# Gated delta layer and gated MLP on one core: weights kept for eight steps, a ring of four places for k, 32x32 blocks through DRAM, and a first phase of three stages with two sets of tiles

## The reference

```python
x = x + layernorm(attn(layernorm(x)))
x = x + layernorm(mlp(layernorm(x)))

# attn, 32 heads, key and value width 64
q, k, v, z = split(x @ w_qkvz.T);  b, a = split(x @ w_ba.T)
q, k, v = causal_conv4(q, k, v)            # depthwise, 4 taps
g = -exp(A_log) * softplus(a + dt_bias);   beta = sigmoid(b)
q = l2norm(q) / 8;  k = l2norm(k)
for t in range(256):                       # state S: 64 x 64 per head
    S = S * exp(g[t])
    S = S + outer(k[t], (v[t] - k[t] @ S) * beta[t])
    o[t] = q[t] @ S
out = (rmsnorm(o) * norm_weight * sigmoid(z)) @ w_out.T
# mlp
out = (silu(h @ w_gate.T) * (h @ w_up.T)) @ w_down.T
```

## Time and profile before

| | |
|---|---|
| runs | 3611.32, 3615.00, 3629.64 us; median 3615.0 |
| profiled execution | 3628.41 us, its span 3626.6 us |
| first phase | 0 to about 159 us |
| second phase | about 169 to 3235 us |
| third phase | to the end |
| busy share of the span | PE 91%, PEld 61%, DVE 69%, ACT 49%, POOL 30% |
| mean granted PE clock | 0.961 of full speed |
| moved by DMA | 351 MB in 930,158 packets, 857,712 of them under 512 bytes |

### The profile page before, as it was taken

One profiled execution on the slowest core, in us unless ns is written; L12 is line 12 of the kernel. 1 busy time (PEld: TensorE's weight loads), 2 busy tenths in 40 slices (PEclk: granted clock), 3 DMA queues, 4 the chain that ended last, 5 costly groups with the idle time before them and its releaser, 6 DMA issues. The chain is left out here.

```text
span 3626.6 us, 117234 instructions
## 1 busy us (share of the span) xinstructions
PE 3284.2 (91%) x51008; PEld 2221.8 (61%) x51008; DVE 2486.1 (69%) x5826; ACT 1769.1 (49%) x3338; POOL 1093.2 (30%) x902
## 2 busy tenths in 40 slices
PE   4489999999999999999999999999999999869998
PEld 2246666666666666666666666666666666645554
DVE  5467767777777777777777777776776777635555
ACT  2245555555555555555555545554555555423333
POOL 0043333333333333333333333333333333300000
PEclk7689999999999999999999999999999999969999
DMA  2235445444544444444444444444444454320000
GB/s 76 75 91 112 113 112 113 113 113 113 113 113 104 103 108 108 106 104 112 104 113 113 113 113 113 113 113 103 110 113 91 109 115 98 87 71 18 24 24 18
DMA packets 930158, 351.24 MB, mean 97 GB/s; under 512 B 857712, under 2 KB 878576, under 8 KB 921328
## 3 DMA queue, kind: packets, MB, share of 16 engines
q1 hardware_dynamic: 929648, 343.73, 40.3%
HBM read 240.35 MB, written 61.34 MB: 83 GB/s over the span
## 5 line engine op out<-in xcount | busy, mean ns | idle before, releaser
L1134 PE MATMUL bank<-xT,w_sb 128*128 128x512 f32 x2048 | 1023.0, 623 | 22.0 <-DMA w_sb<-in_w_qkvz 17.5
L678 POOL TENSOR_TENSOR kq<-kq,products 128x510 f32<-128x510 f32 (+2 forms) x384 | 445.0, 1165 | 941.9 <-ACT kq L752 656.6
L1134 PEld LDWEIGHTS bank<-xT,w_sb 128*128 128x128 f32 x2048 | 350.3, 190 | 309.5 <-issue 253.6
L930 DVE SCALAR_TENSOR_TENSOR kq<-bank,cw,kq 128x510 f32<-128x510 f32 (+2 forms) x384 | 286.6, 746 | 203.9 <-ACT kq L752 189.3
L666 POOL TENSOR_TENSOR dec_a<-gcrow,gccol 128x1024 f32<-128x1024 f32 x64 | 121.8, 1904 | 1001.1 <-DMA beta<-beta_d 1001.1
L1162 PE MATMUL bank<-kq 64*64 64x128 f32 x4096 | 280.7, 278 | 13.2 <-issue 11.4
L930 DVE SCALAR_TENSOR_TENSOR v_c<-bank,cw,v_c 128x510 f32<-128x510 f32 (+2 forms) x384 | 285.2, 743 | 9.0
L948 DVE TENSOR_TENSOR x_un<-x_un,prod_un 128x15 f32<-128x15 f32 (+7 forms) x960 | 258.1, 269 | 32.9
L944 DVE TENSOR_TENSOR prod_un<-a_un,x_un 128x15 f32<-128x15 f32 (+7 forms) x960 | 255.8, 266 | 29.9 <-DMA a_un<-a_d 3.3
L1255 PE MATMUL bank<-wo,u_sq 128*128 128x256 f32 x1024 | 261.4, 399 | 2.8 <-DVE u_sq L1007 2.8
L1162 PEld LDWEIGHTS bank<-kq 64*64 64x64 f32 x4096 | 237.2, 137 | 19.1 <-issue 19.1
(11 more groups left out here) (135 smaller groups left out, 6148.2 us busy)
## 6 DMA issues: line engine op xcount, KB each, us to landing
w_sb<-in_w_qkvz SPq DMA_DIRECT2D x64, 1024.0 KB, 7.9
xT<-xT_d SPq DMA_DIRECT2D x64, 512.0 KB, 5.4
gcrow<-gcrow_d SPq DMA_DIRECT2D x128, 256.0 KB, 5.5
a_d<-a_mat SPq DMA_DIRECT2D x128, 256.0 KB, 3.9
k_old<-kq SPq DMA_DIRECT2D x64, 512.0 KB, 3.8
z_t<-z_d SPq DMA_DIRECT2D x128, 256.0 KB, 4.6
x_row<-x_d SPq DMA_DIRECT2D x128, 256.0 KB, 4.5
wo<-in_w_out SPq DMA_DIRECT2D x64, 256.0 KB, 3.2
```

The source lines that it names most:

```text
L678: nc.gpsimd.tensor_tensor(t[:, :, d:SEQ], t[:, :, d:SEQ], prod[:, :, 0:SEQ - d], ALU.add).then_inc(tap_added[i], 1)
L930: ins = nc.vector.scalar_tensor_tensor(t[:, :, d:SEQ], src[:, :, 0:SEQ - d], cw[:, w:w + 1], t[:, :, d:SEQ], ALU.mult, ALU.add)
L1134: ins = nc.tensor.matmul(bank[:, :], w_sb[:, h, s * P:(s + 1) * P], xT[:, h, :], start=(h == 0), stop=(h == HT - 1))
```

## The change

1. **Weights.** `w_two`, `cw_two` and `wo` have two places, by the parity of the head group. `weights(g)` loads all three once per group, issued two steps before the group starts (group 0 in the first phase). `scale_wo` runs once per group. `xT` has two places too, and `load_x` loads it alone, with no wait of its own.
2. **k.** `kq` becomes one tile of six planes: k of step m in plane m mod 4, q in plane 4 + m mod 2. `keep_k` and `k_old` are gone; `key_state` reads k where it was written, and `scores` takes k and q with a stride between planes.
3. **Blocks.** The scratch tensors `a_d`, `z_d`, `x_d` hold only the 32x32 diagonal blocks. `units_out`, `z_back` and `x_back` are four DMAs each instead of two, with rows of 32 floats (128 bytes), for `x_back` 16 rows of 16 floats per block; `units_in`, `z_out` and `x_out` are one DMA instead of two, and `x_out` stores only the upper 16x16 block of each 32x32. gccol and beta come in one DMA (`gcb`).
4. **First phase.** `spans` runs 10 turns; in turn t, span t is normalised, span t - 1 is projected and gets its gates, and span t - 2 is turned and summed. Most tiles have two places (the banks of the turned x too). beta is computed on ACT as `exp(-ln(1 + exp(-b)))` with a clamp on DVE; the copies of beta to `btc` move from DVE to ACT. The load of x is issued ahead of the constants. Zeros are stored to `z_d` only, at the start; POOL clears `z_t` and `x_row` in SBUF. The first weights are loaded in this phase.

```diff
@@ second phase, SP
+                    def weights(g):
+                        if g > 1:
+                            for k in range(2):
+                                sp.wait_ge(op_full[k], NSP * (g - 1))
+                        sp.dma_start(w_two[g % 2][:, :, :].rearrange("p h t -> p (h t)"), w_qkvz[g]).then_inc(w_in, 16)
+                        sp.dma_start(cw_two[g % 2][:, :], conv_w[g]).then_inc(cw_in, 16)
+                        sp.dma_start(wo[g % 2][:, :, :].rearrange("p a h -> p (a h)"), w_out[g]).then_inc(wo_in, 16)
+
+                    def load_x(m):
+                        sp.dma_start(xT[m.par][:, :, :].rearrange("p h t -> p (h t)"), xT_d[m.index() % NSP]).then_inc(x_T_in[m.par], 16)
+                        if m.off % NSP == NSP - 2 and m.grp + 1 < NHG:
+                            weights(m.grp + 1)
...
                     def units_out(m):
-                        for h in range(2):
-                            sp.dma_start(whole(a_d, h), a_mat[m.par][D * h:D * h + D, :, :]) \
-                                .then_inc(a_d_out, 16)
+                        for q in range(4):
+                            c = W2 * (q % 2)
+                            sp.dma_start(rows32(a_d, q), a_mat[m.par][W2 * q:W2 * q + W2, :, c:c + W2]).then_inc(a_d_out, 16)
...
                     def z_back(m):
-                        for h in range(2):
-                            sp.dma_start(z_t[m.par][D * h:D * h + D, :, :], whole(z_d, h)).then_inc(z_in, 16)
+                        for q in range(4):
+                            c = W2 * (q % 2)
+                            sp.dma_start(z_t[m.par][W2 * q:W2 * q + W2, :, c:c + W2], rows32(z_d, q)).then_inc(z_in, 16)
...
                     def x_back(m):
-                        for h in range(2):
-                            sp.dma_start(x_row[D * h:D * h + D, :, :], whole(x_d, h)).then_inc(x_row_in, 16)
+                        for q in range(4):
+                            c = W2 * (q % 2)
+                            sp.dma_start(x_row[W2 * q:W2 * q + B, :, c:c + B], rows32(x_d, q)[0:B, :, 0:B]).then_inc(x_row_in, 16)
...
                     def turn(s):
                         if s[3]:
                             identity_in(s[3])
-                        if s[2]:
-                            wait_for(sp, conv_done[5], s[2], 1, back=1)
-                            wait_for(sp, tap_done[5], s[2], 1, back=1)
-                            load_cw(s[2])
-                        if s[3]:
                             wait_for(sp, mats_done[0], s[3], 1)
                             units_out(s[3])
                         if s[2]:
                             wait_for(sp, qg_done[1], s[2], 1, back=1)
                             load_gates(s[2])
                         if s[3]:
-                            wait_for(sp, a_d_out, s[3], 32)
+                            wait_for(sp, a_d_out, s[3], 64)
                             units_in(s[3])
                             wait_for(sp, zt_done, s[3], 1)
                             z_out(s[3])
-                            load_wo(s[3])
-                            keep_k(s[3])
                             x_out(s[3])
-                            wait_for(sp, z_d_out, s[3], 32)
+                            wait_for(sp, z_d_out, s[3], 16)
                             z_back(s[3])
-                            wait_for(sp, x_d_out, s[3], 32)
+                            wait_for(sp, x_d_out, s[3], 16)
                             x_back(s[3])
                         if s[1]:
-                            wait_for(sp, proj_full[7], s[1], 1, back=1)
-                            load_xw(s[1])
+                            load_x(s[1])
@@ second phase, places of k and q
+            def half_of(m, q):
+                return kq[:, 4 + m.par if q else m.off % 4, :, :]
```

More of the change, by code:

```diff
@@ L175, in gated_delta_sandwich @@
         sp_gate = sem("sp_gate")
+        w_in, cw_in, wo_in = (sem(n) for n in ("w_in", "cw_in", "wo_in"))
         pool_gate = sem("pool_gate")
@@ L217, in gated_delta_sandwich, with spans @@
+            def spans(turn):
+                for t in range(TURNS):
+                    turn(t if t < NSP else None, t - 1 if 0 <= t - 1 < NSP else None, t - 2 if t >= 2 else None)
             with nc.Block() as block:
@@ L273, in _ @@
[L273 removed]
+                    sp.dma_start(w_two[0][:, :, :].rearrange("p h t -> p (h t)"), w_qkvz[0]).then_inc(w_in, 16)
+                    sp.dma_start(cw_two[0][:, :], conv_w[0]).then_inc(cw_in, 16)
+                    sp.dma_start(wo[0][:, :, :].rearrange("p a h -> p (a h)"), w_out[0]).then_inc(wo_in, 16)
+                    sp.wait_ge(zeros, 3)
+                    for q in range(4):
+                        sp.dma_start(rows32(z_d, q), z_t[0][W2 * q:W2 * q + W2, :, 0:W2]).then_inc(zeros_out, 16)
@@ new lines, in turn @@
+                    def turn(j, k, i):
+                        if j is not None:
+                            if 1 <= j < NSP - 1:
+                                load(j + 1)
+                            store_norm(j)
+                        if i is not None:
+                            store_gates(i)
+                    spans(turn)
+                    sp.wait_ge(eye_in, 32)
+                    sp.wait_ge(zeros_out, 64)
+                    sp.wait_ge(const_in, CONSTS)
+                    for i in range(2):
+                        sp.wait_ge(xT_out[i], 8 * NSP)
+                        sp.wait_ge(col_out[i], 16 * NSP)
+                        sp.wait_ge(row_out[i], 8 * NSP)
@@ new lines, in betas, with rows @@
+                    def betas(i):
+                        act.wait_ge(tok_copied, i + 1)
+                        wait(act, col_out[i % 2], 32 * (i // 2))
+                        for h in range(2):
+                            half = slice(D * h, D * h + D)
+                            nc.scalar.copy(btc[i % 2][half, :, :], tok[i % 2][half, :, h:NH:2].rearrange("p c h -> p h c"))                                 .then_inc(btc_copied, 1)
+                    def rows(i):
+                        act.wait_ge(gc_ready, 2 * i + 2)
+                        wait(act, row_out[i % 2], 16 * (i // 2))
+                        nc.scalar.copy(gcr[i % 2], banks[5][0:NH, :]).then_inc(row_copied, 1)
@@ new lines, in turn @@
+                    def turn(j, k, i):
+                        if k is not None:
+                            magnitudes(k)
+                        if j is not None:
+                            turned(j)
+                        if i is not None:
+                            betas(i)
+                        if k is not None:
+                            gates(k)
+                        if i is not None:
+                            rows(i)
+                        if j is not None and j < NSP - 1:
+                            deviations(j + 1)
@@ L378, in rows @@
-                    def rows(i):
-                        act.wait_ge(gc_ready, 2 * i + 2)
-                        wait(act, row_out, 16 * i)
-                        nc.scalar.copy(gcr, banks[5][0:NH, :]).then_inc(row_copied, 1)
-                    def turn(i):
-                        gates(i)
-                        deviations(i + 1)
-                        turned(i + 1)
-                        rows(i)
-                    deviations(0)
-                    turned(0)
-                    turn(0)
@@ L392, in _ @@
-                    for i in range(1, NSP - 1):
-                        turn(i)
-                    gates(NSP - 1)
-                    rows(NSP - 1)
+                    spans(turn)
                 @block.tensor
```

441 lines of the change are left out of this document (214 added, 227 removed).

## The result

The kernel after takes 3399.74 us (median of 4 runs, 3395.45 to 3404.11) beside 3622.32 us for the kernel before on the same chip (4 runs, 3611.32 to 3630.67). The ratio is 0.9387, with a 95% interval of 0.9354 to 0.9421. The profiled execution took 3400.17 us, its span is 3398.1; against the 3628.41 of before that is 228 us less, where I forecast 169. Direction and order of the parts were right, and the time lies in the range, but only 5 us above its lower end of 3395: the size was too small by 59 us, and the time is nearly that of the rival *all gaps go* (3393), which had a chance of 0.12.

A forecast was written before the change was run, and what follows sets the result against it. Chained engines bound the first phase, PE the second; 3628.4 - 70 (first phase) - 7 (junction) - 92 (second-phase loads) = 3459. The profiled execution lay 13.4 us over the median, so the median forecast was 3446, range 3395 to 3530.

The forecast's parts named there:

- all gaps go: Rival, chance 0.12: halved bytes also relieve L1200 in the second phase, and the first phase runs at 7 us: 3393.
- First phase: Three stages and two tiles overlap the spans: period 17.8 to 8.5 us, 70 us saved (bounds 38 and 88).
- Junction: Between the first phase's end and the second's first matmul: 16.8 us down to 10, 7 saved (0 to 9).
- Second phase, loads: Without weights, `wo` and k copy, L1182 gaps go in seven turns of eight: 92 us saved (0 to 132).
- "quiet" turn: Second-phase turn of 45.00 us in the old trace, where the mean was 46.84; a normal turn would come to 45.1.
- L1200 gaps: PE's second-phase issue gaps under `a_d` and `gcrow` traffic, which keeps its rows: expected to stay, 0.36 us a turn.
- one longer turn in eight: Second phase: the eighth turn stays at today's mean of 46.8 us, the others at 45.1: mean 45.3.
- Gaps stay: Rival, chance 0.22: the queue of small rows, not the weights, makes second-phase instruction blocks late: 3523.
- SyncE's order: Second phase: reordered `z_back` and `units_out`, four DMAs each, would not make PE or DVE wait: nothing gained or lost.
- slower: Rival, chance 0.04: small second-phase DMAs issue slowly and land late, PE waits 7 us a turn at L1173: 3958.
- The `rhs` wait: PE's wait for `rhs` in every second-phase turn, 1.02 us: expected to stay unchanged at 1.0.

The follow-up runs named there:

- a_blocks: Kernel after with the old block transfers put back (rows of 64 floats, two DMAs each), all else as after: 3465.60 us against 3399.74.
- a_recip: Kernel after with beta again by reciprocal on DVE in the three-stage first phase: 3425.94 us in one run, 26 more than after.
- b_first: Kernel before with only the new first phase, old second phase kept: 3551.02 us, 78 less than the 3628.67 of before.
- b_inc16: Kernel before with 16 more semaphore increments at the start of each PE turn: 3740.93 us in one run, 112 more than before.
- a_w: Kernel after with 42 more 1 MB loads of the next group's weights, right behind the load of xT: 3442.51 us against 3399.74.
- a_quiet: Kernel after with 42 more 1 MB weight loads, issued once `a_un` has landed, about 29 us after the `rhs` wait: 3398.35 us.
- b_w: Kernel before with the 1 MB of projection weights loaded only in each group's first step; `wo`, `cw`, k copy kept: 3560.30 us, 68 less.
- a_kcopy: Kernel after with one more DMA per step, copying the step's k (512 KB) to a DRAM scratch tensor: 3397.01 us against 3399.74.
- b_blocks: Kernel before with only the block transfers of the change; weights every turn and copy of k kept: 3575.16 us, 54 less than before.
- a_rows: Kernel after with z's 32x32 blocks read twice more in 35 of 64 turns (4096 rows of 128 bytes, 512 KB): 3403.36 us against 3399.74.

## Why the prediction was right, and where its size was off

The range was met, its mechanism only in part. That PE's gaps are late instruction blocks behind full queues was right. That the weights, with `wo` and the copy of k, bring the whole gain was not, and the range held because it reached down to the rival *all gaps go*, whose reason (halved bytes also relieve L1200) is what a_blocks shows.

- **First phase, forecast 70.** Saved were 158.6 - 83.0 = 75.6, as the period came to 7.8 instead of 8.5. The clock rose to 0.88, not to 1.00, and DVE was busy 6.0 us of a period (38.41 / 50 x 7.8) where I had 6.5. That the reciprocal had to leave DVE for this is shown by a_recip: with it the period is 10.4, DVE's own load, and 22 us of the gain are lost.
- **Junction, forecast 7.** Saved were 16.8 - 7.7 = 9.1, just over its upper bound of 9. It waits for xT, as forecast. Together 84.7 for my 77; b_first gives 83.5 by the same rows and 78 by its times.
- **Second phase, loads, forecast 92.** This is the term that was mis-sized: by the 60 turns it measured 2.17 x 60 = 130, my upper bound of 132. Its first part, that seven turns of eight come down to 45.1, was too short a way: the turns went to 44.7, under the "quiet" turn of 45.00 of the earlier trace rows, which still had a gap (0.38 us at L1200). The shortest turn is 44.37 to 44.39 in all kernels whose turns were taken, but for before (44.56) and b_inc16 (46.92, with its increments). The second, that the L1200 gaps stay because `a_d` and `gcrow` keep their rows, was wrong: they went from 17.7 to 2.6 us, and the old blocks bring them back (16.8 us in a_blocks), the weights don't (2.7 in a_w). The third, "one longer turn in eight", hardly exists: of the seven turns with weights only four have a gap, of 0.4 to 1.5 us. And 143.9 - 130 = 14 us more came outside the 60 turns, 2 ahead of them and 11 behind, which I had not counted: the phase has 67 turns, and seven more at 2.17 would be 15.
- **The cause.** That late instruction blocks stall PE while the queues are full was right (b_inc16, a_w against a_quiet). That the weights, with `wo` and the copy of k, were the whole of it was wrong: the weights alone gave 0.87 of 2.11 us a turn (b_w), the copy of k costs nothing (a_kcopy), and the blocks, which the sum had given nothing, bring 0.53 (b_blocks) or 0.88 (a_blocks). *Gaps stay* is refuted: the gaps went with 81% of the packets still there, and a_rows adds 143,000 for nothing. But the block transfers that it blamed do have about half of the effect, where they stand.
- **SyncE's order, forecast nothing.** Held: four `z_back` DMAs take 1.92 us to issue (991.66), PE's first use of `z_t` is at 1000.61, and no wait for `z_t` shows. The rival *slower* needed 2.9 us for each (four are 11.6 us, not the 11.8 of the text, which changes nothing). The Trainium skill ("DMA: Bandwidth & Descriptors", Specifications) states that pieces under 512 bytes do not reach line rate. Here rows of 128 instead of 256 bytes, half the bytes, land 2.5 us after their issue where it was 4.6, for DMAs of 64 instead of 256 KB; no run kept the bytes and changed the row alone.
- **The `rhs` wait** stayed at 1.0, and 175.67 MB moved for the 180 forecast.

## What to carry to other kernels

A gap "issue" in the middle of like matmuls, which moves on by a fixed number from turn to turn, was here a late block of instructions; some instructions more in each turn, and a shift that changes with them, are the test. Then look at what the DMA queues do just before, and at how fast the engine uses up its instructions there: try moving large transfers to where instructions last long, before cutting them. When several transfers make one train, removing one of them removes only a share of the gaps, so credit each part with that, look at each dense stretch by itself, and take the floor from the shortest turn rather than from a typical good one. Count the slow clock behind a gap too: here it was 0.63 us a turn beside 1.40 of gaps. And a busy engine's wait that stands in every turn of a fixed order may be cheaper than what replaces it: moving the work that ends it made two others.

## What was not expected of the hardware

- Sixteen semaphore increments in a row on PE cost 1.75 us a turn, 0.11 us each, where sixteen 64x64 matmuls with their weight loads take 0.68 us.
- 44 MB of weights in 42 loads cost 43 us or nothing, by their place in the turn; 34 MB of copies and 143,000 more rows of 128 bytes cost nothing.
- The first `rstd` operation of DVE (L307, 128x4) took 3.75 us at 6.60 in the kernel after, and 0.17 us one span later. It ended at 10.35, when POOL's clearing of `acc` in SBUF did (6.93 us from 3.40). Whether the one held up the other was not tried.
